# Two mixing steps joined into one and two narrow corrections joined into one of 272 columns, in a four-layer low-rank residual kernel

## The reference, cut to what matters

```python
x = x + x @ W0.T + 0.5 * (x @ A0[label0[b]]) @ B0.T
x = x + x @ w_eff.T                       # quantised weight plus low-rank part
x = x + x @ W2.T + 0.5 * (x @ A2[label2[b]]) @ B2.T
logits = x @ Wr.T + 5 * one_hot(label7[b])       # 8 experts
gates  = softmax of the two largest logits, 0 elsewhere
h      = x @ A3                                  # 8 experts * 16
out    = x + x @ W3.T + 2 * (h * gates) @ B3
```

## Time and profile before

| what | value |
|---|---|
| median of 3 runs | 607.76 us (607.49 to 609.41) |
| the profiled execution | 607.86 us |
| its span, first to last instruction | 606.1 us |
| PE busy | 600.0 us, 99% of the span |
| PE weight loads | 536.4 us, 89% |
| DVE / ACT / POOL busy | 391.9 / 214.4 / 79.7 us (65 / 35 / 13%) |
| granted TensorE clock, mean | 1.00 of full speed (2.4 GHz) |

### The profile page before, as it was taken

The page is one execution under the profiler, slowest core; times in us unless marked ns, Lnnn a source line. Parts: engine busy times, 40 slices in busy tenths (PEclk is TensorE's granted clock), DMA queues, the critical chain, the costliest instruction groups (busy, mean ns, idle before and its releaser), DMA issues.

```text
span 606.1 us, 9230 instructions
## 1 busy us (share of the span) xinstructions
PE 600.0 (99%) x3247; PEld 536.4 (89%) x3247; DVE 391.9 (65%) x727; ACT 214.4 (35%) x403; POOL 79.7 (13%) x111
## 2 busy tenths in 40 slices
PE   8999999999999999999999999999999999999998
PEld 7999999899999999888888788788888888888887
DVE  3488998999989829200004598967474747475653
ACT  3434233346233129211111278433333333333330
POOL 2101010023000000000000005040404040303120
PEclk9999999999999999999999999999999999999999
DMA  9963220362000030200001110222131313030301
GB/s 263 263 164 92 100 72 1 43 199 89 1 1 1 1 36 1 45 1 0 0 0 35 40 30 1 50 91 79 60 88 50 96 43 109 30 121 17 101 4 71
DMA packets 57824, 37.69 MB, mean 62 GB/s; under 512 B 26684, under 2 KB 51516, under 8 KB 57796
## 3 DMA queue, kind: packets, MB, share of 16 engines
q1 hardware_dynamic: 57796, 37.31, 22.2%
HBM read 28.91 MB, written 8.39 MB: 62 GB/s over the span
## 4 chain that ended last, share of the span: by engine, by line
PE 90%; DVE 7%; ACT 2%; DMA 1%; issue 0%; POOL 0%; POOLq 0%
PE acc L1414 48%; PE acc L1551 29%; PE acc L1572 4%; PE aux L1401 2%; DVE q L1041 2%; PE acc L1574 2%; DVE qtmp L1040 1%; PE acc L1580 1%; PE acc L1581 1%; PE aux L1489 1%; DVE w_lo L945 1%; DVE hg_lo L952 1%; DMA g<-in_L_cond_W_dram 1%; PE acc L1401 1%; ACT hg_hi L611 1%
## 5 line engine op out<-in xcount | busy, mean ns | idle before, releaser
L1414 PE MATMUL acc<-hg_hi,w_hi 128*128 128x352 f32 (+2 forms) x384 | 87.2, 335 | 1.3 <-DVE w_lo L945 0.9
L1414 PE MATMUL acc<-hg_lo,w_hi 128*128 128x352 f32 (+2 forms) x384 | 85.8, 331 | 0.0
L1414 PE MATMUL acc<-hg_hi,w_lo 128*128 128x352 f32 (+2 forms) x384 | 85.6, 330 | 0.0
L1414 PEld LDWEIGHTS acc<-hg_hi,w_hi 128*128 128x128 f32 x384 | 66.3, 188 | 2.9 <-DVE w_lo L945 1.3
L1414 PEld LDWEIGHTS acc<-hg_hi,w_lo 128*128 128x128 f32 x384 | 67.3, 188 | 0.0
L1414 PEld LDWEIGHTS acc<-hg_lo,w_hi 128*128 128x128 f32 x384 | 67.2, 188 | 0.0
L945 DVE TENSOR_TENSOR w_lo<-a_t,w_hi 128x1024 fp32r<-128x1024 f32 (+2 forms) x9 | 9.9, 1105 | 82.1 <-ACT w_hi L603 82.1
L1041 DVE TENSOR_TENSOR q<-q,qtmp 128x1024 f32<-128x1024 f32 x48 | 59.5, 1240 | 1.7
L768 ACT CAST left_hi<-xr 128x512 fp32r<-128x512 f32 x64 | 39.6, 622 | 51.1 <-PE acc L1551 33.6
L539 POOL TENSOR_TENSOR xr<-xr 128x512 f32<-128x512 f32 x28 | 35.7, 1298 | 130.4 <-DVE left_lo L1190 129.1
L1551 PE MATMUL acc<-rh_a,left_hi 128*128 128x512 f32 (+1 forms) x132 | 52.7, 399 | 0.0
(11 more groups left out here) (213 smaller groups left out, 1042.5 us busy)
## 6 DMA issues: line engine op xcount, KB each, us to landing
x_st<-in_x_dram SPq DMA_DIRECT2D x64, 128.0 KB, 2.9
out_dram<-part SPq DMA_DIRECT2D x31, 256.0 KB, 2.8
g<-in_L_cond_W_dram SPq DMA_DIRECT2D x8, 512.0 KB, 7.2
w_st<-in_L_cond_W_dram SPq DMA_DIRECT2D x8, 512.0 KB, 4.6
a_t<-in_L_cond_weight_dram SPq DMA_DIRECT2D x8, 512.0 KB, 5.0
w_raw<-in_L_cond_weight_dram SPq DMA_DIRECT2D x8, 512.0 KB, 4.3
a_raw<-in_L_cond_lora_A_dram SPq DMA_DIRECT2D x5, 128.0 KB, 3.6
a_raw<-in_L_cond_lora_A_dram SPq DMA_DIRECT2D x20, 32.0 KB, 1.9
```

Of the source, the lines that this page charges most:

```text
L1414: last = pe.matmul(acc[0:a.shape[-1], slot, bank * BANK:bank * BANK + c1 - c0], a[:, k, :], b[:, k, c0:c1], start=(at == 0 and n == 0), st ...
```

## The change

- **Mixing.** In pairs 1 to 7 there is one `mix()` for both blocks, in place of `mix(0)` in M2 and `mix(1)` in M4: two matmuls of 256 columns in M4. `vt` and `vm` are one tile each with both blocks side by side, and `m_high` and `m_low` are one instruction of 256 columns each. Pair 0 keeps two mixings.
- **Correcting.** A tile `vbe` holds the high and the low part of the 136 columns for h and logits side by side. `correct_others(h)` is one matmul of 2*136 = 272 columns into both halves of the narrow result. In pairs 1 to 7 both blocks are corrected after M4. `copy_second` therefore copies 64 columns only, and a new `copy_h(h)` (ACT) copies the 136 corrected columns; `best_two(h)` waits for it.
- **Transposes of the gated rows (pairs 1 to 7).** `turn_g(0)` goes from the fourth k-step of M6 to the middle of M5; `turn_g(1)` from the second k-step of M7 to just ahead of the fourth.
- **DVE order (pairs 1 to 7).** `left_low(S1)` goes ahead of `m_low`, `g_low(0)` ahead of `left_low(S4)` and `gated(1)`, `g_low(1)` between the halves of `x_turn(b, 0, 1)`. `x_turn(b, 1, 1)` goes behind the outputs C21 and C22.
- **ACT order (pairs 1 to 7).** `g_high(1)` goes ahead of `left_high(A12)` of the next pair.

```diff
+        vbe = place("vbe", 34752, [P, 2, NR], F32R)
+        vm = place("vm", 37888, [P, 2, P], F32R)
+        AUX_MIX = aux[:, P:3 * P]
...
@@ ACT, vb_high
-                act.copy(vb_hi[half * 2 * R:(half + 1) * 2 * R, :], bp[:, 0:C_LOW2]).then_inc(vb_hd, 1)
+                act.copy(vb_hi[rows, :], bp[:, 0:D]).then_inc(vb_hd, 1)
+                act.copy(vbe[rows, 0, :], bp[:, D:C_LOW2]).then_inc(vb_hd, 1)
...
@@ ACT
-                    act.copy(hl[h][:], E_BANK[h][:, E_W:]).then_inc(second_copied, 1)
+                    act.copy(hl[h][:, 0:EH], E_BANK[h][:, E_W:E_W + EH]).then_inc(second_copied, 1)
+                def copy_h(h):
+                    act.wait_ge(r_done, b * 2 + (h + 1))
+                    act.copy(hl[h][:, EH:], E_BANK[h][:, E_W + EH:]).then_inc(h_copied, 1)
...
@@ ACT, first pair
                     left_high(b, "S1")
+                    copy_h(0)
                     m_high(1)
...
                     done("M4")
+                    copy_h(1)
                     left_high(b, "S4")
@@ ACT, later pairs
                 left_high(b, "S2")
-                m_high(0)
                 v_high(1)
                 done("M2")
                 left_high(b, "S1")
-                m_high(1)
+                m_high()
+                copy_h(0)
+                copy_h(1)
                 exponential(0)
...
                 copy_part("M5", "Z")
+                g_high(1)
                 if ahead:
                     left_high(b, "A12", 1)
-                g_high(1)
                 copy_part("M7", "X")
@@ DVE, later pairs
-                m_low(0)
                 v_low(1)
+                left_low(b, "S1")
+                m_low()
                 best_two(0)
-                m_low(1)
                 gated(0)
-                left_low(b, "S1")
                 best_two(1)
+                g_low(0)
                 left_low(b, "S4")
                 gated(1)
-                g_low(0)
                 if ahead:
-                    x_turn(b, 0, 1)
+                    x_turn(b, 0, 1, (0,))
+                g_low(1)
+                if ahead:
+                    x_turn(b, 0, 1, (1,))
                     sel_low(b + (E_FIRST + 1))
                 out("C11", "Y", "F11", "M1")
                 if ahead:
                     left_low(b, "A12", 1)
-                g_low(1)
-                if ahead:
-                    x_turn(b, 1, 1)
                     left_low(b, "A11", 1)
                 out("C21", "W", "F21", "M7")
                 if ahead:
+                    out("C22", "X", "F22", "M5")
+                    x_turn(b, 1, 1)
                     left_low(b, "A21", 1)
-                    out("C22", "X", "F22", "M5")
                     left_low(b, "A22", 1)
@@ PE
+                    at, rows = (aux_at(h, 1), vt[:, h]) if first else (AUX_MIX, vt[:].rearrange("p h r -> p (h r)"))
+                    pe.matmul(at, tsel_h[:], rows, start=True, stop=False, skip_group_check=True)
+                    pe.matmul(at, tsel_l[:], rows, start=False, stop=True, skip_group_check=True).then_inc(mix_done, 1)
...
-                    pe.matmul(at, vm[h][:], vb_hi[:, D:C_LOW2], start=False, stop=False, skip_group_check=True)
-                    pe.matmul(at, vm[h][:], vb_lo[:, D:C_LOW2], start=False, stop=True,
-                              skip_group_check=True).then_inc(r_done, 1)
+                    at = E_BANK[h].rearrange("p (u c) -> p u c", u=2)[:, :, EH:]
+                    pe.matmul(at, vm[:, h], vbe[:], start=False, stop=True, skip_group_check=True).then_inc(r_done, 1)
...
                 product("X", "S2", "T2", range(3))
-                turn_g(0)
+                if first:
+                    turn_g(0)
                 product("X", "S2", "T2", range(3, HALF)).then_inc(step_done, 1)
...
-                product("Z", "S1", "T1", range(HALF), start=True).then_inc(step_done, 1)
+                product("Z", "S1", "T1", range(2), start=True)
+                if not first:
+                    turn_g(0)
+                product("Z", "S1", "T1", range(2, HALF)).then_inc(step_done, 1)
...
-                product("X", "S3", "T3", range(1))
+                turn_at = 1 if first else 3
+                product("X", "S3", "T3", range(turn_at))
                 turn_g(1)
-                product("X", "S3", "T3", range(1, HALF)).then_inc(step_done, 1)
+                product("X", "S3", "T3", range(turn_at, HALF)).then_inc(step_done, 1)
```

More of the change, by code:

```diff
@@ L250, in aux_at, with gated_at @@
             return aux[:, h * BANK + n * P:h * BANK + (n + 1) * P]
+        AUX_MIX = aux[:, P:3 * P]
+        AUX_GATED = (aux[:, BANK + 2 * P:BANK + 3 * P], aux[:, 3 * P:4 * P])
+        def gated_at(first, h):
+            return aux_at(h, 2) if first else AUX_GATED[h]
         w3_in = [sem(f"w3_in{k}") for k in range(KT)]
@@ L821, in vb_high @@
             def vb_high(half):
[L822 removed]
+                rows = slice(half * 2 * R, (half + 1) * 2 * R)
+                act.copy(vb_hi[rows, :], bp[:, 0:D]).then_inc(vb_hd, 1)
+                act.copy(vbe[rows, 0, :], bp[:, D:C_LOW2]).then_inc(vb_hd, 1)
             act.wait_ge(acc_done, PASSES)
@@ L1177, in sel_low, with x_turn @@
                                   ALU.subtract).then_inc(e_split, 1)
-            def x_turn(b, h, ahead=0):
-                dve.wait_ge(x_in, b * (32 * QUARTERS) + 16 * QUARTERS * (2 * ahead + h + 1))
-                for half in range(2):
+            def x_turn(b, h, ahead=0, halves=(0, 1)):
+                if 0 in halves:
+                    dve.wait_ge(x_in, b * (32 * QUARTERS) + 16 * QUARTERS * (2 * ahead + h + 1))
+                for half in halves:
                     ks = slice(half * HALF, (half + 1) * HALF)
@@ L1262, in v_low, with m_low @@
                     dve.wait_ge(v_hd, b * 2 + (h + 1))
-                    dve.tensor_tensor(vt[2 * R:], aux_at(h, 0)[2 * R:], vt[2 * R:].bitcast(F32),
+                    dve.tensor_tensor(vt[2 * R:, h], aux_at(h, 0)[2 * R:], vt[2 * R:, h].bitcast(F32),
                                       ALU.subtract).then_inc(v_split, 1)
[L1266 to L1269, removed]
+                def m_low(h=None):
+                    if first:
+                        dve.wait_ge(m_hd, h + 1)
+                        low, mixed = vm[2 * R:, h], aux_at(h, 1)
+                    else:
+                        dve.wait_ge(m_hd, b + 2)
+                        low, mixed = vm[2 * R:].rearrange("p h r -> p (h r)"), AUX_MIX
+                    dve.tensor_tensor(low, mixed[2 * R:], low.bitcast(F32), ALU.subtract).then_inc(m_split, 1)
                 def g_low(h):
                     dve.wait_ge(g_hd, b * 2 + (h + 1))
-                    dve.tensor_tensor(hgt_l[h][:], aux_at(h, 2), hgt_h[h][:].bitcast(F32),
+                    dve.tensor_tensor(hgt_l[h][:], gated_at(first, h), hgt_h[h][:].bitcast(F32),
                                       ALU.subtract).then_inc(g_split, 1)
@@ L1579, in finish @@
                     cols, at = slice(half * HD + c.start, half * HD + c.stop), BANKS[bank][:, c]
-                    pe.matmul(at, vm[h][:], vb_hi[:, cols], start=False, stop=False, skip_group_check=True)
-                    pe.matmul(at, vm[h][:], vb_lo[:, cols], start=False, stop=False, skip_group_check=True)
+                    pe.matmul(at, vm[:, h], vb_hi[:, cols], start=False, stop=False, skip_group_check=True)
+                    pe.matmul(at, vm[:, h], vb_lo[:, cols], start=False, stop=False, skip_group_check=True)
                     three(at, (hgt_h[h][:], hgt_l[h][:]), (b3_hi[half][:, c], b3_lo[:, cols]),
@@ L1641, in pair @@
                 product("Y", "A12", "B21", range(1), start=True)
-                mix(0)
+                if first:
+                    mix(0)
                 product("Y", "A12", "B21", range(1, 2))
```

58 lines of the change are left out of this document (30 added, 28 removed).

## The result

| | before | after |
|---|---|---|
| median of 6 runs | 607.76 us (607.35 to 609.41) | 610.67 us (610.29 to 610.96) |
| ratio, 95% interval | | 1.0046 (1.0034 to 1.0057) |
| profiled execution / its span | 607.86 / 606.1 us | 610.29 / 608.5 us |

A forecast was written before the change was run, and what follows sets the result against it. PE's own stream was taken to bound the kernel (busy 600.0 of 606.1 us). Terms -3.1 + 1.9 + 3.5 + 0.1 + 0.4 = +2.8 gave 610.7 us profiled, 610.6 median; range 609.3 to 612.8.

The forecast's parts named there:

- Item 1: Mixing and corrections on PE: fewer short matmuls save 0.44 a pair in seven pairs, -3.1 us.
- Item 4: Before F11: moved `turn_g(0)` and late corrections make one long gate chain that just fits, +0.1 us.
- Item 2: `turn_g(1)` to F21: the later transpose makes F21 wait 0.27 in all seven pairs, +1.9 us.
- Item 3: ACT's queue behind `g_high(1)`: A12 delays the copy of M7, F22 loses 0.59 in six pairs, +3.5 us.
- Item 5: Pair 0: extra `vbe` copies and `copy_h(0)` behind S1 delay DVE, which comes out in PE, +0.4 us.
- only the first wait appears: Rival: A12 is ready anyway, so F21 waits but F22 does not; 607.1 us, chance 0.08.
- its rival: F11 waits too, 0.3 in each of seven pairs; 612.7 us, chance 0.13.
- Item 6: Effects put at nothing: later mixed v, `x_turn(b, 1, 1)` behind C22 with its reload, stores, POOL's sums, clock.

The follow-up runs named there:

- a third: On the kernel before, only the new ACT and DVE orders, with `turn_g(1)` left after the first k-step: 607.35 us, beside 607.43 (ratio 1.0002).
- the experiment with the halves together: On the changed kernel, both halves of `x_turn(b, 0, 1)` put ahead of `g_low(1)` on DVE: 607.00 us (ratio 0.9988 to the kernel before).
- `vbe` later: Changed kernel with M7's copy before A12, `turn_g(1)` after two k-steps, `copy_h(0)` before S1; `vbe` copies and split moved behind those of `c_hi`, `c_lo`: 604.65 us (0.9953).

## Why the prediction was right, step by step

Read between the same two points in both traces, and summed:

| term | predicted | measured in the traces |
|---|---|---|
| joined matmuls with F11 (items 1 and 4) | -3.1 + 0.1 | -3.03 (six pairs at 0.455, pair 1 at 0.30) |
| F21 (item 2) | +1.9 | +1.74 (seven times 0.25) |
| F22 (item 3) | +3.5 | +3.74 (six times 0.62) |
| pair 0 (item 5) | +0.4 | +0.45 |
| sum | +2.8 | +2.9 |

The medians differ by 2.9. From the first matmul of pair 0 to the end the two traces differ by 3.0 (242.4 and 245.4); the 0.1 that the table lacks is F12, which follows the held F22 0.02 to 0.03 later in six pairs. The stage ahead of pair 0 was 0.67 shorter in the profiled execution after the change, which is why the two profiled executions differ by 2.4 only; the other eleven traces place that within its scatter. The mechanism was right in its four larger terms. That the sum hit to 0.1 us is partly luck: F21 was forecast 0.2 too dear and F22 0.2 too cheap.

- **Item 1** is right in size, and that the cost does not go by columns is shown by cutting the joined ones again, which costs 0.42 of the 0.46 of a pair again. The formula of the Trainium skill ("TensorE: Matmul & The Clock Gate", back-to-back issue gap) for an isolated matmul, columns/2.4 plus 2.5 ns, would have made that an estimated +0.1 us in all; 2.5 were measured. The same section says that in a stream the spacing is set by the weight load and the matmul together; a spacing above what the formula gives fits that, though its 81 ns for 128 columns was 110 here (435.13 to 435.24). That it is the weight load which is not hidden was argued and not tested: in the pages of both kernels every matmul has a load of its own.
- **Item 2.** The links of the way around were each at most 0.02 off (the 0.04 from ACT's end to DVE's start, for which the rows of before have no example at `g_low(1)`, measured 0.03), and 0.25 was lost where 0.27 was forecast. The late transpose alone on the kernel before gave this wait and only this.
- **Item 3** is the one that decided the sign. It was found by following a queue, not a price: which instruction stands behind the moved one, what it waits for, and who waits for it. Two experiments each break one of its two links (the order on ACT, the order on DVE), and each removes the whole wait at F22; a third shows that without the late transpose neither link costs anything. The size was 0.62 where 0.59 was forecast: ACT's step from A12 to the copy took 0.53 and not 0.48. The rival "only the first wait appears" needed A12's rows in time, which is what the experiment with the halves together made.
- **Item 4.** In pairs 2 to 7 F11 did not wait, as said. The chain measured 5.80 us in pair 2 (C = 438.14; `g_low(0)` ends at 443.77, with 0.17 for the reaction) and F11 started at C+5.84: 0.04 us in hand, and that was enough. A forecast that rests on so little could as well have gone to its rival.
- **Item 5.** The size is right, its make-up partly. `copy_h(0)` behind S1 was worth 0.34 of the 0.45. PE's wait in front of `turn_v(0)` did not grow, as the prediction had it, but shrank from 0.26 to 0.08, since PE had been held before it, for 0.18, by a step that the prediction did not have: the small split of sel, below. Taking that wait away was worth only 0.05 at F21; the last 0.09 stays open.
- **Item 6.** The reload's cover was real: the experiment that leaves `x_turn(b, 1, 1)` ahead of C22 takes it away, and loses 12 us. The mixed v came in time: no row of PE's waits names it.

## What to carry to other kernels

When an operation is moved on one engine, write down from its new start when each engine hands over, and compare with the work that the bound engine has left there; then do the same for whatever stands *behind* the moved operation in each queue. Here a detour of 1.06 us cost 0.25 a pair, the copy queued behind it 0.62. A place for an operation has two edges: here one k-step was too early by 0.39 us, three too late by 0.25 and 0.62, two cost nothing once the copy of M7 stood first, and the same change, with that place and the copy of M7 one place earlier, became 0.46% faster than the kernel before where it had been 0.46% slower.

## What the runs showed of the hardware that was not expected

In pair 0 of the changed kernel a DVE instruction on 64 columns took 1.33 us, and PE's weight load waited 0.43 us for it. It ran beside a POOL instruction with two inputs. DVE, then POOL, then the weight load, of the changed kernel:

```profile
366.78 1.33 DVE L1199 TENSOR_TENSOR e_all<-sel_raw,e_all 128x64 fp32r<-128x64 f32 x1
```

```profile
366.73 1.29 POOL L585 TENSOR_TENSOR t<-cm,t 128x512 f32<-128x512 f32 x1
```

```profile
368.16 0.19 PEld L1601 LDWEIGHTS acc<-e_all,left_hi 128*128 128x128 f32 x1 [0.43 <-DVE e_all L1199]
```

With `vbe` later, both started within 0.01 us of each other, and the same DVE instruction took 0.21; POOL's took 1.37:

```profile
367.54 0.21 DVE L1199 TENSOR_TENSOR e_all<-sel_raw,e_all 128x64 fp32r<-128x64 f32 x1
```

```profile
367.53 1.37 POOL L585 TENSOR_TENSOR t<-cm,t 128x512 f32<-128x512 f32 x1
```

So it was in the kernel before:

```profile
367.42 0.21 DVE L1176 TENSOR_TENSOR e_all<-sel_raw,e_all 128x64 fp32r<-128x64 f32 x1
```

```profile
367.41 1.36 POOL L575 TENSOR_TENSOR t<-cm,t 128x512 f32<-128x512 f32 x1
```

All thirteen traces fall into these two kinds: in five DVE starts at most 0.01 us after POOL and takes 0.21, in eight 0.04 to 0.05 after it and takes 1.32 or 1.33.

In the changed kernel DVE's instruction started 0.05 us after POOL's and ended 0.09 after it, as if it had been held for all of it. The Trainium skill ("SBUF — State Buffer", who interferes with whom) has the rule: a DVE instruction with two SBUF inputs and a GpSimd one that reads SBUF exclude each other for a whole instruction. The slow rows agree. The fast ones do so only in part: POOL's instruction then took 0.08 longer and not 0.21. The consequence for a prediction: ACT finished the piece that this split reads 0.10 us later, counted from the pair's first matmul (3.73 instead of 3.63), DVE's instruction started 0.04 later, and it ended 1.15 later. Here little of that reached the total, 0.05 us at F21 by the experiment with `vbe` later.
